# Splitting the rows of a GNN edge stage into two f16 halves on ScalarE and GpSimd before the transposes, and the digits of the chunk one-hots by 7 and 14

## The reference

```python
edge_index = stack([src, dst])            # dst is sorted
xn  = layernorm(x)
agg = zeros_like(xn).at[src].set(xn[dst]) # the last edge of a node wins
x   = x + concat(xn, agg) @ W.T + b       # W is 256 x 512
t   = layernorm(x)
probs = softmax(t @ router_w.T)           # 8 experts, the best 2, weights renormalised
x   = x + t + sum over e of combine_e * (gelu(t @ w1[e] + b1[e]) @ w2[e] + b2[e])
```

## Time and profile before

| what | us |
|---|---|
| median of 3 runs | 1154.61 (1147.53 to 1157.86) |
| the profiled execution, its own time | 1151.43 |
| its span in the trace | 1149.7 |
| busy in the span: PE, DVE, ACT, POOL | 834.9, 845.0, 643.0, 601.8 |
| the matmuls L855 of the edge stage, 1600 | 83.4 |
| the high products L1163, 100 | 93.4 |
| first matmul of the edge stage, and the winning chunks ready (L1274) | 20.3, 247.0 |

### The profile page before, as it was taken

The page is one execution under the profiler, slowest core; times in us unless marked ns, Lnnn a source line. Parts: engine busy times, 40 slices in busy tenths (PEclk is TensorE's granted clock), DMA queues, the critical chain, the costliest instruction groups (busy, mean ns, idle before and its releaser), DMA issues.

```text
span 1149.7 us, 28889 instructions
## 1 busy us (share of the span) xinstructions
PE 834.9 (73%) x9319; PEld 707.6 (62%) x9319; DVE 845.0 (73%) x1912; ACT 643.0 (56%) x1743; POOL 601.8 (52%) x669
## 2 busy tenths in 40 slices
PE   1699999996786742343434588888888888888886
PEld 1599999984565631232333377776776766776766
DVE  7999999975776656566978757666666766766666
ACT  4567777753443413443542366676656666766665
POOL 6974454464554467546710145555555555555554
PEclk9899999997878875555555889999999999999999
DMA  8810010025744355354535312221222222122220
GB/s 232 255 59 27 28 36 27 27 69 184 228 144 124 114 160 160 101 164 129 174 115 38 15 57 64 68 67 58 66 63 69 62 65 70 59 69 66 67 57 12
DMA packets 79214, 104.91 MB, mean 91 GB/s; under 512 B 22593, under 2 KB 64538, under 8 KB 78994
## 3 DMA queue, kind: packets, MB, share of 16 engines
q0 software_dynamic: 21408, 54.87, 16.6%
q1 hardware_dynamic: 57714, 48.76, 15.1%
HBM read 63.16 MB, written 44.01 MB: 93 GB/s over the span
## 4 chain that ended last, share of the span: by engine, by line
PE 40%; DVE 19%; issue 14%; another core or an unknown queue 13%; ACT 9%; ACTq 2%; POOL 1%; DMA 1%; DVEq 0%; POOLq 0%; SPq 0%
PE bank L1054 10%; PE bank L1068 7%; PE bank L878 7%; PE bank L855 7%; ACT arena L818 3%; PE bank L890 2%; PE bank L899 2%; PE bank L872 2%; PE bank L1022 2%; ACT arena L779 1%; DVE bst L1360 1%; DVE arena L1343 1%; DVE arena L1163 1%; DVE big L1357 1%
## 5 line engine op out<-in xcount | busy, mean ns | idle before, releaser
L1054 PE MATMUL bank<-arena,w1s 128*128 128x128 f16 x3000 | 210.1, 220 | 78.6 <-issue 70.9
L1054 PEld LDWEIGHTS bank<-arena,w1s 128*128 x3000 | 177.3, 98 | 112.6 <-issue 110.3
L588 POOL DMA_INDIRECT out<-arena,gidx x125 | 141.9, 1135 | 185.7 <-DVE arena L1498 149.8
L818 ACT ACTIVATE arena<-bank,b1s 128x128 f32<-128x128 f32 x500 | 141.6, 367 | 154.4 <-remote 150.4
L1068 PE MATMUL bank<-w2s,arena 128*128 x1500 | 184.0, 273 | 0.7 <-DVE arena L1478 0.7
L577 POOL DMA_INDIRECT arena<-tok_rows,gidx x125 | 123.8, 990 | 107.0 <-DVE gidx L1467 69.1
L878 PE MATMUL bank<-wgs,arena 128*128 128x256 f16 x1176 | 164.0, 295 | 4.3 <-issue 4.3
L1493 DVE SCALAR_TENSOR_TENSOR arena<-bank,arena 128x256 f32<-128x256 f32 x125 | 60.0, 480 | 128.5 <-remote 125.4
L1068 PEld LDWEIGHTS bank<-w2s,arena 128*128 128x128 f16 x1500 | 141.0, 98 | 16.5 <-DVE arena L1478 0.9
L878 PEld LDWEIGHTS bank<-wgs,arena 128*128 128x128 f16 x1176 | 123.7, 106 | 34.3 <-issue 7.0
L561 POOL DMA_INDIRECT arena<-key_rows,cid x98 | 94.7, 966 | 82.4 <-DVEq L1292 47.2
(11 more groups left out here) (229 smaller groups left out, 1611.0 us busy)
## 6 DMA issues: line engine op xcount, KB each, us to landing
agg_rows<-arena SPq DMA_DIRECT2D x49, 256.0 KB
tok_rows<-arena SPq DMA_DIRECT2D x13, 896.0 KB
big<-x SPq DMA_DIRECT2D x5, 1792.0 KB, 13.9
arena<-w SPq DMA_DIRECT2D x16, 256.0 KB, 2.8
big<-x SPq DMA_DIRECT2D x6, 512.0 KB
arena<-tok_rows,gidx POOLq DMA_INDIRECT x125
out<-arena,gidx POOLq DMA_INDIRECT x125
arena<-key_rows,cid POOLq DMA_INDIRECT x98
```

What stands on the lines that cost most here:

```text
L588: gp.indirect_dma_start(out, bass.IndirectOffsetOnAxis(gidx[:, j:j + 1], 0), ob[:, j % DEPTH, :], None, bounds_check=N - 1, oob_is_err=Fal ...
L818: last = sc.activation(h32[:, u % 2, at:at + P], bank[2 + u % 2][:, at:at + P], ACT.Gelu, bias=b1s[:, ds(e[x], 1), f], scale=1.0 / SCALE)
L1054: last = mm(bank[2 + u % 2][:, at:at + P], parts[x, w, c, f], a[:, u % 4, c * P:(c + 1) * P], start=(n == 0), stop=(n == 5))
```

## The change

The high digits are split by 7 and 14 in place of 4 and 25, so `oh_1` has 7 entries, `oh_2` 14 and `oh_hi` 98. The four operations of `high_products` become one, on 6272 elements. In the edge stage the normalised rows are split before they are transposed: ACT copies `xn` to f16 (`high_rows`, into `rowh`), POOL subtracts (`low_rows`, into `rowl`), and PE transposes both with 8 f16 matmuls (`node_halves`) in place of 8 f32 ones and the matmul with the negative identity. ACT's `take_low` waits for `xt_ready`. The pairs after the edge stage are transposed as before.

```diff
-H1, H2 = 4, 25
+H1, H2 = 7, 14
@@ POOL
+            def low_rows(p, k):
+                pool.wait_ge(rowh_ready, p + 1)
+                gp.tensor_tensor(rowl[:, k, :], xn[:, k, :, :].rearrange("p a d -> p (a d)"), rowh[:, k, :],
+                                 ALU.subtract).then_inc(rowl_ready, 1)
...
             gp.tensor_tensor(wgs[:, 1, :, :].rearrange("p a b -> p (a b)"), wgf,
                              wgs[:, 0, :, :].rearrange("p a b -> p (a b)"), ALU.subtract).then_inc(wgs_ready, 1)
+            low_rows(0, 0)
             early_norm(2, 0)
+            low_rows(1, 1)
             pool.wait_ge(s_edges, 64)
...
             early_norm(3, 1)
+            low_rows(2, 0)
...
             for p in range(4, PA):
                 early_norm(p, p % 2)
+                if p <= ND - 1:
+                    low_rows(p - 1, (p - 1) % 2)
@@ ACT
+            def high_rows(i, k):
+                act.wait_ge(xn_ready, 2 * i + 2)
+                sc.activation(rowh[:, k, :], xn[:, k, :, :].rearrange("p a d -> p (a d)"), ACT.Copy).then_inc(rowh_ready, 1)
...
             def take_low(i, k, first):
-                act.wait_ge(rest_ready, i + 1)
+                act.wait_ge(xt_ready, i + 1)
...
                     normalise(d, k)
+                if not known or d < ND - 1:
+                    high_rows(d, k)
@@ PE
+            def node_halves(i, k, first):
+                pe.wait_ge(rowl_ready, i + 1)
+                if not first:
+                    pe.wait_ge(xl_ready, i)
+                for to, rows in ((bank[k], rowh), (bank[7], rowl)):
+                    for n in range(4):
+                        last = mm(to[:, n * P:(n + 1) * P], rows[:, k, n * P:(n + 1) * P], identh[:, :], start=True, stop=True)
+                last.then_inc(xt_ready, 1)
...
-            def node_rest(i, k, first=False):
...
-                if not known or 0 <= i + 1 < T // 2:
-                    node_transposes(i + 1, 1 - k, known and i + 1 < 2)
+                if groups and (not known or i + 1 >= 0):
+                    node_halves(i + 1, 1 - k, known and i + 1 < 1)
+                elif not groups and i + 1 < T // 2:
+                    node_transposes(i + 1, 1 - k, False)
                 if not known or i >= 0:
                     node_linear(i, k, known and i < 2, groups)
-                if groups and (not known or i + 1 >= 0):
-                    node_rest(i + 1, 1 - k, known and i + 1 < 1)
@@ DVE
             def high_products():
-                for a in range(H1):
-                    last = ve.tensor_tensor(oh_hi[:, :, a * H2:(a + 1) * H2, :], oh_2,
-                                            oh_1[:, :, a:a + 1, :].broadcast_to([CH, GC, H2, 2]), ALU.mult)
-                last.then_inc(onehots_ready, 1)
+                shape = [CH, GC, H1, H2, 2]
+                ve.tensor_tensor(oh_hi.rearrange("p c (a b) q -> p c a b q", a=H1), oh_2.unsqueeze(2).broadcast_to(shape),
+                                 oh_1.unsqueeze(3).broadcast_to(shape), ALU.mult).then_inc(onehots_ready, 1)
```

More of the change, by code:

```diff
@@ L195, in gnn_moe @@
         xn = one.take([P, 2, 2, D], f32)
+        rowh = one.take([P, 2, 2 * D], f16)
+        rowl = one.take([P, 2, 2 * D], f16)
         xh = one.take([P, 2, 2 * D], f16)
@@ L279, in gnn_moe @@
         xn_ready, xt_ready, xh_ready, xl_ready = sem("xn_ready"), sem("xt_ready"), sem("xh_ready"), sem("xl_ready")
-        rest_ready, w_high = sem("rest_ready"), sem("w_high")
+        rowh_ready, rowl_ready, w_high = sem("rowh_ready"), sem("rowl_ready"), sem("w_high")
         g_ready, self_added, agg_copied = sem("g_ready"), sem("self_added"), sem("agg_copied")
```

## The result

The changed kernel took 1171.26 us (median of 4 runs, 1169.08 to 1179.89), the kernel before 1151.95 (4 runs, 1147.53 to 1157.86): ratio 1.0174, interval 1.0120 to 1.0228. It is slower, by about 19 us; the profiled span went from 1149.7 to 1168.5.

What follows compares the result with a forecast made beforehand. PE was taken to bound the step at 8.66 us, DVE's own work just below at 8.46. +7 in the beginning and +6.5 in the steps, on 1151.4, gave 1165, plus 3.2 for the median: 1168 us, range 1146 to 1179.

Steps and rivals of the forecast that it cites:

- PE's part: Edge-stage step on PE: f16 transposes replace 2.06 us by 0.50, so PE needs 7.10 us for 8.66 and idles 1.9.
- DVE's part: Edge-stage step on DVE: single product 3.31 us for 3.61, smaller digit operations; step 8.02 us without POOL's cost.
- rival 4: DVE's single product loses its rate with another access pattern: +80 us, 1235 us; chance 0.03.
- POOL's price (the port): Each POOL subtraction in the edge stage costs DVE 1.00 us, as the two engines take turns.
- Rival 1: POOL's subtraction costs DVE nothing: edge step 8.02 us, time 1143 to 1146 us; chance 0.15.
- Steady step: Edge-stage step of 9.02 us for 8.66, +0.36 in each of 18 steps, +6.5 us together.
- The beginning: First edge steps: PE waits for POOL ahead of the transposes of step 4, +2 to +10 us, taken as +7.
- Rival 3, the clock: PE's clock falls in each steady step's idle time: 0.3 us a step lost, +5, 1173 us; chance 0.12.

Runs made afterwards that it cites:

- experiment 3: Changed kernel with POOL's subtraction replaced by a memset of the same tile, low halves left out of the result: 968.73 us, ratio 1.0017 to the kernel before.
- 4: Changed kernel without POOL's subtraction; PE forms the low halves from f32 transposes less the high rows in bank 7: 966.89 us, ratio 0.9986 to the kernel before.
- 11: Kernel of experiment 4 with POOL's keys spread over the first norms and its affine selects over norms 8 to 16: 1142.55 us, ratio 0.9898 to the kernel before.
- experiment 2: Changed kernel with digits 4 and 25 and four products again, rows still split by ACT and POOL: 1010.26 us, ratio 1.0426 to the kernel before.
- 1: Kernel before with only the digits 7 and 14 and the single product, rows and transposes unchanged: 975.94 us, ratio 1.0084 to the kernel before.
- experiment 7: Kernel of experiment 4 with digits 4 and 25 and four products: 1209.92 us, ratio 1.0496 to the kernel before.
- 12: Kernel of experiment 4 with digits 4 and 25, but the product as one operation of 6400 elements: 1146.88 us in one run.
- 8: Kernel of experiment 4 with POOL's keys and affine selects moved behind the norms: 1150.81 us, ratio 0.9954 to the kernel before.
- 6: Changed kernel with POOL's keys behind the low rows of pair 2 and affine selects behind all norms: 1170.07 us, ratio 1.0165 to the kernel before.

## Why the prediction was right

The time and the range held (1168 forecast, 1171.26 measured), and so did what sets the steady step. The closeness is in part luck: the sum forecast +13.5 for the profiled execution and +18.8 was measured, and 3.2 of the 1168 were the distance of a median of three from one profiled time, which was 0.5 with the fourth run. The cause of the loss in the beginning was only partly right. By its own steps:

- **PE's part: right.** The transposes took 0.61 in the row, 0.44 from start to start, for 0.50; PE stands idle 1.75 us a step for 1.9.
- **DVE's part: right.** 3.33 us from product to product's successor for 3.31, and 8.02 for the whole of DVE's own work (experiments 3, 4, 11). The single product keeps its rate, so rival 4 falls.
- **POOL's price (the port): right, 0.96 for 1.00.** The earlier trace rows had it: the same engine pair at nearly the same number of columns. Rival 1 falls by the rows of the change, and experiment 3 shows what it would have needed: a POOL operation that doesn't read. The estimate of 1.11 from the 2.6 cycles an element of the Trainium skill, page "GPSIMD Engine Reference", section "Elementwise — side-by-side cycle accounting", is of POOL's own time; the trace has 1.16 for that, for the subtraction at 75.41, beside which DVE stood still, and the price that DVE paid is smaller.
- **Steady step: 8.98 for 9.02**, 5.9 us for 6.5.
- **The beginning: +9.5 and +7.2 in two executions, for +7.** The size held, its place was wrong, so the size is in part luck. The prediction had PE wait ahead of the transposes of step 4, behind the affine selects. PE waited in steps 1 and 3; a wait ahead of the transposes of step 4 (9.54) showed only in experiment 3. The step that failed is the claim that the three earlier subtractions held up nobody: it put them into POOL's queue with 3.0 us together, asked for none of them whether PE waits for it, and let only the affine selects stretch beside the long product. But the subtraction of pair 0 stood behind the split of the weights and came at 43.78, so PE waited 11.35 (8.61 in the second execution). And the keys stretched just so (9.85 for 5.38), and the subtraction of pair 2, in line behind them, waited for the product to end (4.33). With DVE standing still, POOL then made the affine selects good quickly, which is why step 4 had no wait.
- **A part I left out:** the last subtraction falls beside the maxima, +0.96. Another 2.7 us lie behind the edge stage; whether they come from the change or are scatter no run tells.
- **Rival 3, the clock:** did not come in the steady steps (1.75 us of idle, clock 1.00). In experiment 2 it came eight times, seven behind 2.2 us of idle and one behind 1.91. So the forecast's 1.9 was near to it.

What my theory did not weigh: a delay in the beginning does not need the subtraction. Experiments 1, 4 and 3 are 6.5, 8.1 and 10.4 us late there with a cheap POOL part or none. In 1 and 4 the long product holds up POOL's affine selects and two-column operations, and through the norm of pair 5 ACT, PE and DVE. The prediction had the long product hold up the affine selects, but only ahead of a subtraction. Experiments 7 and 12 show the product's part: they differ only in it. Moving POOL's work (8 and 11) let the step's gain reach the chunks. How much of the changed kernel's own loss would stay without the subtraction isn't shown, since PE waits there at other places. Moving POOL's work in it (6) did not help: 11.0 us of PE's wait in step 1 stayed, the keys prolonged DVE's work elsewhere, and the end waited for the selects.

## What to carry to other kernels

Before work is given to POOL because POOL is idle, count what it reads while DVE runs two-input operations: here every subtraction of 512 columns cost DVE 0.96 us, more than the whole change saved it. Where two engines stand at 8.66 and 8.46 a step, relieve both in one edit and check a third by its queue, since a longer operation on one delays short ones on the other. The best version took the subtraction to PE, which had just the room once half of its transposes were f16 (8.05 us for DVE's 8.02), and spread POOL's one-off work between the norms that others wait for.

## What the runs showed of the hardware

- Some two-column operations of POOL took as long as DVE's single product beside them (3.25 to 3.33 us), and four took 25.36 us where DVE ran its two-input operations, the product in four, without a pause (experiment 7).
- A POOL operation of 512 columns cost DVE 0.00 us as a memset, 0.40 as an f16 copy and 0.96 as a subtraction with an f32 and an f16 input.
- The same 64 matmuls took 3.04 to 3.06 or 4.53 to 4.64 us (granted clock 1.00, or 0.50 for some 3 us of it) behind idle times of 1.82 to 2.24 us in experiment 2, the longer time mostly behind 2.2. In the changed kernel they once took 3.08 behind 2.49. So the length of the idle time alone doesn't tell whether the clock falls.
- The same kernel took 967 us on one chip and about 1151 on the others. The difference lies behind the edge stage. No run here tells why.
